# The heads' gathered tiles due 2.2 a step for 48 steps and 1.1 a step after, instead of 1.4 a step throughout

## What is computed

```python
xn = _layernorm(x)
neigh_sum  = segment_sum(xn[src], dst, 6250)          # edges: gather a row, add it to its node
gnn  = normalize(relu(concat([xn, neigh_sum / deg]) @ W + b))
mix  = _layernorm_gamma(linear_attention(xn), gamma)  # k softmax over nodes, q softmax per head
x    = x + gnn + mix
tokens = _layernorm(x)
# top 2 of 8 experts for each token, gelu MLP of each, weighted sum
x = x + tokens + sum(weight[e] * (gelu(tokens @ w1[e] + b1[e]) @ w2[e] + b2[e]))
```

## Time and profile before

| | |
|---|---|
| median of 3 runs | 1911.18 us (1910.07 to 1914.4) |
| profiled execution, device time | 1922.39 us |
| its span | 1920.6 us |
| its mean granted TensorE clock | 0.914 of full speed |
| TensorE / VectorE / ScalarE / POOL busy | 81% / 57% / 40% / 62% of the span |
| first gather of the last stage (tile 702) | 1081.3 us from the start |
| first scatter of cohort 0 | 1213.7 us |
| TensorE's first work on job 0 | 1269.8 us |

### The profile page before, as it was taken

One profiled execution on the slowest core, in us unless ns is written; L12 is line 12 of the kernel. 1 busy time (PEld: TensorE's weight loads), 2 busy tenths in 40 slices (PEclk: granted clock), 3 DMA queues, 4 the chain that ended last, 5 costly groups with the idle time before them and its releaser, 6 DMA issues.

```text
span 1920.6 us, 33157 instructions
## 1 busy us (share of the span) xinstructions
PE 1547.5 (81%) x10026; PEld 1206.0 (63%) x10026; DVE 1088.0 (57%) x3833; ACT 775.6 (40%) x1935; POOL 1181.3 (62%) x1154
## 2 busy tenths in 40 slices
PE   2398888898888999999996577549867895888794
PEld 2166666666657988888884355437656674666563
DVE  9655555555656776767761388826544772562202
ACT  4633333333333444444441000026434453566573
POOL 2477767667674787777777776564476555315313
PEclk9999999999998999999997666769888997898897
DMA  6666666566653434434445475345456654544535
GB/s 220 201 191 201 197 192 196 183 186 203 190 183 112 118 114 124 122 115 118 122 127 161 132 224 155 119 124 180 145 168 205 200 166 142 176 141 148 164 108 159
DMA packets 206516, 308.74 MB, mean 161 GB/s; under 512 B 31099, under 2 KB 150312, under 8 KB 206344
## 3 DMA queue, kind: packets, MB, share of 16 engines
q0 software_dynamic: 54864, 149.89, 27.2%
q1 hardware_dynamic: 132328, 139.29, 22.5%
q10 hardware_dynamic: 19152, 17.44, 2.6%
HBM read 213.85 MB, written 92.65 MB: 160 GB/s over the span
## 4 chain that ended last, share of the span: by engine, by line
PE 49%; POOL 14%; DMA 10%; DVE 10%; issue 8%; ACT 5%; SPq 3%; ACTq 1%; POOLq 0%; DVEq 0%
POOL sb_ring L800 10%; PE ps_zone L927 6%; PE ps_zone L925 6%; PE ps_proj L989 4%; PE ps_hidden L996 4%; PE ps_zone L880 4%; POOL sent_tokens L833 4%; PE ps_zone L882 4%; PE ps_expert L913 4%; PE ps_hidden L1120 3%; PE ps_turned L889 2%; PE ps_expert L1131 2%; DMA out<-sb_bias_row 2%; PE ps_hidden L913 2%; DMA out<-sb_arena 2%
## 5 line engine op out<-in xcount | busy, mean ns | idle before, releaser
L800 POOL DMA_INDIRECT sb_ring<-xn_table,sb_idx x947 | 978.3, 1033 | 460.4 <-issue 324.7
L1569 DVE TENSOR_TENSOR sb_lo_onehot<-sb_iota,sb_lo_pairs 128x256 f16<-128x256 f16 x616 | 177.9, 289 | 292.5 <-PE ps_expert L913 203.5
L927 PE MATMUL ps_zone<-sb_arena,sb_adjacency 128*121 128x257 f16 x1372 | 333.7, 275 | 0.0
L925 PE MATMUL ps_zone<-sb_arena,sb_adjacency 128*121 128x256 f16 x1372 | 332.7, 273 | 0.0
L880 PE MATMUL ps_zone<-sb_ring,sb_onehot 128*128 128x256 f16 x947 | 245.3, 290 | 62.0 <-DMA sb_ring<-xn_table,sb_idx 36.3
L1569 DVE TENSOR_TENSOR sb_key_onehot<-sb_iota_key,sb_rel 128x528 f16<-128x528 f16 (+1 forms) x616 | 267.9, 435 | 0.0
L882 PE MATMUL ps_zone<-sb_ring,sb_onehot 128*128 128x257 f16 x947 | 246.6, 291 | 0.0
L1225 ACT ACTIVATE sb_adjacency<-ps_expert 128x264 f16<-128x264 f32 (+1 forms) x410 | 168.9, 421 | 191.7 <-PE ps_expert L913 189.3
L925 PEld LDWEIGHTS ps_zone<-sb_arena,sb_adjacency 128*121 128x121 f16 x1372 | 185.9, 135 | 14.8 <-issue 5.3
L927 PEld LDWEIGHTS ps_zone<-sb_arena,sb_adjacency 128*121 128x121 f16 x1372 | 185.1, 135 | 6.5 <-issue 6.5
L880 PEld LDWEIGHTS ps_zone<-sb_ring,sb_onehot 128*128 128x128 f16 x947 | 99.0, 105 | 120.1 <-DMA sb_ring<-xn_table,sb_idx 54.8
(11 more groups left out here) (241 smaller groups left out, 2662.2 us busy)
## 6 DMA issues: line engine op xcount, KB each, us to landing
sb_stage<-sent_tokens SPq DMA_DIRECT2D x133, 128.0 KB, 2.3
answers<-sb_stage ACTq DMA_DIRECT2D x133, 128.0 KB
sent_tokens<-sb_zeros SPq DMA_DIRECT2D x43, 384.0 KB, 4.3
sb_ring<-xn_table,sb_idx POOLq DMA_INDIRECT x947, 3.1
keys_values<-sb_stage SPq DMA_DIRECT2D x49, 256.0 KB, 2.3
queries_selves<-sb_stage SPq DMA_DIRECT2D x49, 256.0 KB, 2.3
sb_stage<-keys_values SPq DMA_DIRECT2D x96, 128.0 KB, 2.7
sb_arena<-queries_selves SPq DMA_DIRECT2D x24, 512.0 KB, 4.2
```

What stands on the lines that cost most here:

```text
L800: pool.indirect_dma_start(ring3[:, place, 0:2 * D], None, table, bass.IndirectOffsetOnAxis(tile_idx, 0)).then_inc(signal, 16)
L925: pe.matmul(set_sum[0:SET_ROWS, 0:D], adj3[:, h, :], rows16[:, h, 0:D], start=h == 0, stop=False, skip_group_check=True)
L927: mm = pe.matmul(set_sum[0:SET_ROWS, 0:D + 1], adj3[:, h, :], rows16[:, h, D:2 * D + 1], start=False, stop=h == BLOCKS - 1, skip_group_che ...
L1569: return dve.tensor_tensor(to.rearrange("p t (c two) -> p t c two", two=2), numbers.rearrange("p (c two) -> p c two", two=2).unsqueeze(1). ...
```

## The change

`MAIN_RATE` goes from 1.4 to 1.1 tiles a step, and the first 48 steps get a rate of their own, 2.2. Nothing else is edited.

```diff
-MAIN_RATE = 1.4
+EARLY_STEPS, EARLY_RATE, MAIN_RATE = 48, 2.2, 1.1
@@ main_steps
-    count = [0] + [min(GATHER_TILES - MAIN_TILE, int(MAIN_RATE * (k + 1))) for k in range(heads)]
+    count = [0] + [min(GATHER_TILES - MAIN_TILE, int(EARLY_RATE * min(k + 1, EARLY_STEPS) + MAIN_RATE * max(k + 1 - EARLY_STEPS, 0))) for k in range(heads)]
```

## The result

The changed kernel takes 1928.11 us (median of 10 runs, 1919.53 to 1930.1), the kernel before 1912.79 beside it (10 runs): a ratio of **1.0065, with a 95% interval of 1.004 to 1.0089**, or +12.4 us of 1912.8 (+7.7 to +17.0). The ratio goes by the means of the two sets, 1926.5 and 1914.1 us; their medians stand 15.3 us apart. The forecast was +13.0.

What follows compares the result with a forecast made beforehand. The prediction took the path to run through POOL's in-order queue of gathers and scatters, with 17.5 us of slack before the first scatter. 29.1 - 11.8 - 4.3 = +13.0 us on 1911.2 gave 1924.2 us, range 1911 to 1936.

Steps and rivals of the forecast that it cites:

- What bounds: Before the first scatter: POOL issues 37 more gathers at 1.272 us without pause, making that scatter 29.1 us late.
- Dearer gathers: Rival, chance 0.13: gathers with their gap cost 1.33 us, first scatter 36.5 us late, time 1931.6 us.
- `dispatch`: Before the first scatter: the rows of dispatch are there by 1238.5, 4 us before POOL, so gathers end last.
- The rounds: POOL's three rounds of scatters: nine gathers fewer at 1.31 us give -11.8 us, all of which counts.
- TensorE in the late steps, -4.3: From step 68 on: 32 fewer tiles to sum, 17 of them on the path at 0.25 us each.
- The sum: Whole kernel: 29.1 - 11.8 - 4.3 = +13.0 us.
- the delay: At the first scatter: +29.1 us, with bounds of +26.4 and +32.6.
- the give-back: After the first scatter: -11.8 us from fewer gathers among scatters and -4.3 us from fewer late tiles on TensorE.
- Faster: Rival, chance 0.11: from step 68 on, late tiles at 0.52 us outweigh the early wait, time 1905.8 us.
- no change: Rival, chance 0.10: all 32 late tiles count at 0.43 us, +1 to +4 us, time 1912 to 1915 us.
- The rule of the Trainium skill on interleaving regimes: First heads and late steps: by it alone, moved tiles would be free early, a gain of -16.1 us.

Runs made afterwards that it cites:

- experiment 9: The changed kernel with 1.9 tiles a step over the first 48 steps and 1.2 after: ratio 0.998 (0.995 to 1.0009) to the kernel before.
- experiment 1: The changed kernel with 1.6 tiles a step over the first 48 steps and 1.3 after: ratio 0.995 (0.9931 to 0.9969) to the kernel before.
- experiment 2: The changed kernel with POOL asked for tiles only 4 ahead, not 16, up to step 63: ratio 1.0018 (0.9993 to 1.0043) to the kernel before.
- experiment 3: The kernel before, with POOL's lead shrinking from 16 to 4 tiles over each of the three rounds of scatters: ratio 0.9795 (0.9755 to 0.9836).
- experiment 4: The kernel before, with both TensorE products of the 150 tiles from step 68 on issued twice: ratio 1.0047 (1.0025 to 1.0068).
- Experiment 6: The kernel before, with VectorE making each batch of one-hots twice from step 68 on: ratio 1.0005 (0.9976 to 1.0034).
- experiment 10: The kernel before, with no tiles due in steps 64 to 67 and all later ones due four steps later: ratio 0.998 (0.9954 to 1.0005).

## Why the prediction was right, and where its sum was not

*What bounds.* POOL's queue ahead of the first scatter, as predicted: 126 intervals of 1.280 us (predicted 1.272), no wait on the ring, the wait for `dispatch` gone. The first scatter is 30.3 and 29.8 us late, predicted 29.1, and the sum holds at a second rate (experiment 9, 144.1 for 143.8), while within the slack nothing moves (experiment 1). Both limits of the first scatter go back to the rate at which POOL issues gathers: POOL's queue, and the heads that wait for tiles (experiment 2).

*Dearer gathers*, the rival at 1931.6, are out: from tile 702 on the mean gather takes 0.977 us after and 0.979 before. The 1.033 of the earlier trace rows, from which that rival had its price, is a mean of the whole kernel, and it holds 29 gathers of more than 1.5 us, all of them ahead of the last stage. The longest, in before, stands beside a run of VectorE, nearly all one-hots, without a pause (timeline of POOL and DVE):

```profile
624.30 5.68 POOL L800 DMA_INDIRECT sb_ring<-xn_table,sb_idx  x1 [0.30 <-issue]
...
628.71 0.46 DVE L1569 TENSOR_TENSOR sb_key_onehot<-sb_iota_key,sb_rel 128x552 f16<-128x552 f16 x1
...
630.29 0.95 POOL L800 DMA_INDIRECT sb_ring<-xn_table,sb_idx  x1 [0.30 <-PE ps_zone L882]
```

It ends 0.8 us after the last one-hot of that run, and so do 19 of the 29. This agrees with the rule of the Trainium skill ("SBUF — State Buffer", "SBUF: two separate sides") that VectorE can lock POOL out of writing descriptors. So the prediction looked for it in too few rows: the trace shows gathers held up in this way, but ahead of the last stage. In this stage, with VectorE busy 70% (81.56 of 117 us), no gather ahead of the first scatter takes more than 1.36 us, and a gather with its gap stays at 1.28 us. No run tried which of VectorE's instructions hold a gather up.

*`dispatch`.* The prediction has the first scatter free to go at 157.2 behind 702, 4 us ahead of POOL. The rows were written at 153.4 and 155.0, which with the 1.0 us from the rows to the scatter in before is 6 to 8 us ahead of POOL. The step from the router products of pair 5 to the rows took 19.2 and 20.0 us, where before it took 23.7; the prediction had carried that over. Pairs took 18.4, 20.1, 22.4, 22.3 and 23.2 us: the 22.4 of the prediction from pair 3 on, less at first. TensorE took no tile from 1074.60 (tile 701) to 1084.22 (tile 702), so that POOL began the stage 11 us ahead and not 2.8, and this head start was used up in pairs 1 and 2.

*The rounds.* 46.9 and 45.7 us for the two later ones, predicted 47.2 and 46.3. Nearly all of it counts, as experiment 3 shows at almost four times the size (39 of 44 us).

*TensorE in the late steps, -4.3.* This is the term that was mis-sized. Its price, 0.25 us for a tile by the row of two starts, is what a tile takes on TensorE, not what the path loses: measured by experiment 4, 0.06 us net, so 32 tiles would be 2 us. Yet more came back: 6.2 and 4.5 us in steps 68 to 99 alone, where I had 2.5. Experiment 6 excludes VectorE's one-hots, experiment 10 has the stretch 7 us shorter with the same tiles placed four steps later, with a granted clock of 0.96 for 0.91. So what gave the time back is open: the clock is a reading that two other profiles don't bear out, and what keeps it up isn't settled either, since experiment 10 moved the zones' turns, the gathers and TensorE's pauses together, and no run moved one of them alone.

*The sum.* After the second round's end the two profiles of after differ by up to 12 us, so of the last terms only the third round can be read (-5.8 and -5.6, predicted -5.2). The total, +12.4, is near the +13.0 partly because the delay was 1 us more than predicted and the give-back about as much; as the give-back came for a reason that the prediction did not have, that closeness is in part luck. In experiment 9 the same sum fails by that term: a first scatter 11.7 us late, and no loss at the end.

*The rivals on the other side.* "Faster" and "no change" needed a late tile of 0.43 us and more, and fall by experiment 4. The rule of the Trainium skill on interleaving regimes ("Perfetto Trace Analysis", "Optimization Strategy") predicted a gain. At 2.2 a step the runs show +0.65%, at 1.9 -0.2% (-0.5 to +0.09), at 1.6 -0.5% (-0.7 to -0.3): a gain is shown only where POOL, which feeds the idle regime, still has time to spare.

## What to carry to other kernels

Before work is moved into a stretch where the bound engine is idle, count the slack of the queue that feeds it, in issue intervals, up to the first thing that others wait for: here 17.5 us, 13 gathers, and the change put 37 there. With 23 (experiment 9) the first scatter was late by what the count says, but the end was not, so the count gives the delay and not yet the price. In a queue that issues in order, work that can wait and stands between a producer and what the bound engine waits for is paid nearly in full: taking 33 gathers out of the scatters' rounds gave 2.05%, and with a rate inside the slack 2.75%, far more than moving TensorE's products could.

## What the runs showed of the hardware that was not expected

TensorE's busy time and its price are far apart: 84 busy us of extra products cost 9 us, though TensorE looks 92% busy in the first stretch where they stand. Almost the same list of products took 108.0 and 100.8 us as its tiles stood four steps apart, with the granted clock at 0.91 and 0.96 (one profile of each). A gather that takes POOL 0.95 us took up to 5.68 us beside VectorE's one-hots without a pause. And two executions of the same program, within 1.3 us of each other at the marks of the table for 365 us of the last stage, then differ by 10 us, from the first finished blocks on.
